# Mixture of experts with two towers on one core: order of the transfers and of the gates around the first expert's second layer

## What is computed

```python
h = relu(einsum('bi,eio->beo', x, eW1) + eb1)      # x: 512 x 1024, eW1: 8 x 1024 x 1024
h = relu(einsum('beh,eho->beo', h, eW2) + eb2)     # eW2: 8 x 1024 x 512
expert_out = einsum('beh,eho->beo', h, eW3) + eb3  # eW3: 8 x 512 x 256
gates = softmax(einsum('bi,tie->bte', x, gW) + gb, axis=-1)   # 2 tasks, 8 experts
tin = einsum('bte,bed->btd', gates, expert_out)
th = relu(einsum('btd,tdh->bth', tin, tW1) + tb1)
th = relu(einsum('bth,tho->bto', th, tW2) + tb2)
out = sigmoid(einsum('bth,tho->bto', th, tW3) + tb3)[..., 0]  # 512 x 2
```

## Time and profile before

| | |
|---|---|
| median of 3 runs | 576.89 us (575.41 to 577.55) |
| profiled execution | 576.8 us, span 575.0 us |
| mean granted clock of TensorE | 0.997 |
| TensorE busy | 567.6 us, 99% |
| VectorE busy | 454.9 us, 79% |
| ScalarE busy | 310.7 us, 54% |
| GpSimd busy | 99.8 us, 17% |
| moved by DMA | 86.87 MB, 151 GB/s on average |

### The profile page before, as it was taken

The page is one execution under the profiler, slowest core; times in us unless marked ns, Lnnn a source line. Parts: engine busy times, 40 slices in busy tenths (PEclk is TensorE's granted clock), DMA queues, the critical chain, the costliest instruction groups (busy, mean ns, idle before and its releaser), DMA issues.

```text
span 575.0 us, 8534 instructions
## 1 busy us (share of the span) xinstructions
PE 567.6 (99%) x2883; PEld 478.4 (83%) x2883; DVE 454.9 (79%) x576; ACT 310.7 (54%) x422; POOL 99.8 (17%) x106
## 2 busy tenths in 40 slices
PE   9999989999999999999999999999999999999998
PEld 6788878888888888888888888888888888888776
DVE  7998559976898758976799759977699767998493
ACT  3484546724764365633665346733757346654553
POOL 0200411033201511033100431024110332004000
PEclk9999989999999999999999999999999999999999
DMA  9824784368635765466744577266744676416100
GB/s 322 225 85 149 186 210 101 136 161 232 152 106 170 190 155 142 146 165 164 201 97 154 149 201 178 77 183 184 165 125 146 164 186 185 122 73 204 52 1 0
DMA packets 39774, 86.87 MB, mean 151 GB/s; under 512 B 3521, under 2 KB 8769, under 8 KB 39762
## 3 DMA queue, kind: packets, MB, share of 16 engines
q1 hardware_dynamic: 29762, 66.50, 34.4%
q0 software_dynamic: 9856, 19.96, 20.3%
q10 hardware_dynamic: 144, 0.26, 0.2%
HBM read 86.68 MB, written 0.04 MB: 151 GB/s over the span
## 4 chain that ended last, share of the span: by engine, by line
PE 84%; DVE 3%; DMA 2%; issue 2%; ACT 1%; POOL 1%; ACTq 0%; POOLq 0%; DVEq 0%
PE psum L487 31%; PE psum L490 16%; PE psum L347 12%; PE psum L348 12%; PE psum L349 12%; DMA w_raw<-eW_pairs 2%; DVE w_lo L998 1%; DVE h_lo L1014 1%; POOL scratch L1414 0%; DVE scratch L1091 0%; ACT w_hi L953 0%; ACT h_hi L819 0%; ACT scratch L988 0%; DVE scratch L1069 0%; POOL gates_dram L1417 0%
## 5 line engine op out<-in xcount | busy, mean ns | idle before, releaser
L998 DVE TENSOR_TENSOR w_lo<-w_raw,w_hi 128x1024 fp32r<-128x1024 f32 (+2 forms) x108 | 137.8, 1280 | 19.2 <-ACT w_hi L782 12.0
L347 PE MATMUL psum<-h_hi,w_hi 128*128 128x512 f32 (+1 forms) x340 | 131.8, 388 | 0.8 <-DVE h_lo L1014 0.8
L487 PE MATMUL psum<-t_both,w_hi 128*128 128x512 f32 x480 | 131.6, 396 | 0.0
L348 PE MATMUL psum<-h_lo,w_hi 128*128 128x512 f32 (+1 forms) x340 | 131.6, 387 | 0.0
L349 PE MATMUL psum<-h_hi,w_lo 128*128 128x512 f32 (+1 forms) x340 | 131.4, 387 | 0.0
L487 PE MATMUL psum<-x_both,w_hi 128*128 128x512 f32 x360 | 98.7, 396 | 2.2 <-ACT scratch L803 2.2
L487 PEld LDWEIGHTS psum<-t_both,w_hi 128*128 128x128 f32 x480 | 83.1, 190 | 11.6
L1401 POOL DMA_DIRECT2D w_raw<-eW_pairs x30 | 25.9, 865 | 343.8 <-DMA w_raw<-eW_pairs 343.1
L1014 DVE SCALAR_TENSOR_TENSOR h_lo<-scratch,h_hi 128x512 fp32r<-128x512 f32 (+1 forms) x66 | 66.8, 1013 | 23.4 <-ACT scratch L845 19.0
L490 PEld LDWEIGHTS psum<-t_both,w_lo 128*128 128x128 f32 x480 | 73.8, 189 | 10.3
L490 PE MATMUL psum<-t_both,w_lo 128*128 128x256 f32 x480 | 76.4, 281 | 0.0
(11 more groups left out here) (100 smaller groups left out, 582.2 us busy)
## 6 DMA issues: line engine op xcount, KB each, us to landing
w_raw<-eW_pairs SPq DMA_DIRECT2D x30, 768.0 KB, 4.2
w_raw<-eW SPq DMA_DIRECT2D x40, 512.0 KB, 4.0
scratch<-eW_pairs SPq DMA_DIRECT2D x30, 256.0 KB, 4.8
w_raw<-eW_pairs SPq DMA_DIRECT2D x30, 256.0 KB, 5.1
w_raw<-eW_pairs POOLq DMA_DIRECT2D x30, 256.0 KB, 4.9
scratch<-eW_pairs POOLq DMA_DIRECT2D x30, 256.0 KB, 6.5
scratch<-gates_dram POOLq DMA_DIRECT2D x8, 512.0 KB, 5.6
w_raw<-tW SPq DMA_DIRECT2D x4, 512.0 KB, 4.2
```

Source lines behind the costliest of these rows:

```text
L347: pe.matmul(bank, weights_hi, moving_hi, start=first, stop=False)
L348: pe.matmul(bank, weights_hi, moving_lo, start=False, stop=False)
L487: pe.matmul(whole, weights(w_hi, kk), moving(kk), start=(starts and kk == 0), stop=False, skip_group_check=True)
L998: dve.tensor_tensor(wide(w_lo, slots), raw, wide(w_hi, slots).bitcast(F32), ALU.subtract).then_inc(slot_ready, 1)
```

## The change

Four things are done together.

1. GpSimd issues the accumulating DMAs of (1,1) right behind those of (1,0), ahead of the memsets and the gates' trip.
2. SyncE orders the blocks of (1,0) behind the low part of piece 0 instead of piece 1. For that, piece 1 moves from raw unit 0 to unit 3, piece 2 to unit 2, and piece 3 to unit 3 behind piece 1, so it is ordered once the low part of piece 1 is done.
3. `turn_gates` moves on TensorE from ahead of layer 2 of expert 0 to behind P4 of pair 3, inside it.
4. VectorE's order around it is another one.

```diff
-FIRST_W2_UNIT = [1, 0, 3, 2]
+FIRST_W2_UNIT = [1, 3, 2, 3]
+FIRST_PER_UNIT = [1 + FIRST_W2_UNIT.count(u) for u in range(UNITS)]
...
@@ sync @@
-            for n, what in enumerate([("G3", 2), ("G4", 2), ("G3", 3), ("G4", 3)]):
-                sp.wait_ge(slot_ready, split(0, *what))
-                load_w2(0, n)
-
-            sp.wait_ge(slot_ready, split(0, "W2", 1))
+            sp.wait_ge(slot_ready, split(0, "G3", 2))
+            load_w2(0, 0)
+            sp.wait_ge(slot_ready, split(0, "G3", 3))
+            load_w2(0, 1)
+
+            sp.wait_ge(slot_ready, split(0, "W2", 0))
             load_blocks(1, 0)
             load_a22(1, 0)
+            sp.wait_ge(slot_ready, split(0, "G4", 3))
+            load_w2(0, 2)
+            sp.wait_ge(slot_ready, split(0, "W2", 1))
+            load_w2(0, 3)
@@ tensor @@
                     if first and (n, m) == (2, 0):
                         last_product(e, PAIRS - 1)
+                        turn_gates()
...
             pair(0, 3)
-            turn_gates()
             layer2(0)
@@ scalar @@
                     u = FIRST_W2_UNIT[i]
-                    act.wait_ge(landed[u], 2 * DMA)
+                    act.wait_ge(landed[u], (1 + FIRST_W2_UNIT[:i + 1].count(u)) * DMA)
...
@@ vector @@
             upper_fold(0, 2)
             lower_fold(0, 2)
+            w2_lo(0, 0)
             c11_sum(0, 3)
...
-            w2_lo(0, 0)
+
             g4_lo(0, 3)
+            c12_sum(0, 3)
+            c21_fold(0, 2)
+            c22_sum(0, 3)
+            pair_h1_lo(0, 2)
+            w2_lo(0, 1)
+
             dve.wait_ge(exp_done, 1)
...
-            c12_sum(0, 3)
-            c22_sum(0, 3)
-            c21_fold(0, 2)
-            pair_h1_lo(0, 2)
-            w2_lo(0, 1)
+            upper_fold(0, 3)
+            lower_fold(0, 3)
             w2_lo(0, 2)
             dve.wait_ge(gates_turned, 1)
             dve.tensor_copy(turned[0:T * E, :], banks[BANK_GATES][0:T * E, :]).then_inc(gated_ready, 1)
-            upper_fold(0, 3)
-            lower_fold(0, 3)
             c21_fold(0, 3)
@@ gpsimd @@
             sum_blocks(1, 0)
+            sum_blocks(1, 1)
 
             pool.wait_ge(t_ready, NX)
...
-                for i in range(1, PAIRS):
+                for i in range(2 if e == 1 else 1, PAIRS):
```

More of the change, by code:

```diff
@@ L821, in w3_split @@
             def w3_split(e):
-                act.wait_ge(landed[W3_UNIT], (2 + PER_UNIT[W3_UNIT] * (e - 1) + 1) * DMA)
+                act.wait_ge(landed[W3_UNIT], (FIRST_PER_UNIT[W3_UNIT] + PER_UNIT[W3_UNIT] * (e - 1) + 1) * DMA)
                 wait_slots(e, W3_AT, 2)
@@ L828, in w2_hi @@
                     u = FIRST_W2_UNIT[i]
-                    act.wait_ge(landed[u], 2 * DMA)
+                    act.wait_ge(landed[u], (1 + FIRST_W2_UNIT[:i + 1].count(u)) * DMA)
                 else:
                     u = W2_UNIT[i]
-                    act.wait_ge(landed[u], (2 + PER_UNIT[u] * (e - 1) + W2_UNIT[:i + 1].count(u)) * DMA)
+                    act.wait_ge(landed[u], (FIRST_PER_UNIT[u] + PER_UNIT[u] * (e - 1) + W2_UNIT[:i + 1].count(u)) * DMA)
                 wait_slots(e, W2_AT + 2 * i, 2)
@@ L940, in _ @@
                 w2_hi(e, 3)
-            act.wait_ge(landed[LAST_W3_UNIT], (2 + PER_UNIT[LAST_W3_UNIT] * (E - 1) + 1) * DMA)
+            act.wait_ge(landed[LAST_W3_UNIT], (FIRST_PER_UNIT[LAST_W3_UNIT] + PER_UNIT[LAST_W3_UNIT] * (E - 1) + 1) * DMA)
             act.wait_ge(out3_done, OUT3 * (E - 1))
@@ L947, in tower_hi @@
                 u = TOWER_UNIT[i]
-                act.wait_ge(landed[u], (2 + PER_UNIT[u] * (E - 1) + (2 if u == LAST_W3_UNIT else 1)) * DMA)
+                act.wait_ge(landed[u], (FIRST_PER_UNIT[u] + PER_UNIT[u] * (E - 1) + (2 if u == LAST_W3_UNIT else 1)) * DMA)
                 if i < 3:
```

## The result

The changed kernel took 572.88 us (median of 10 runs, 572.65 to 573.45); the kernel before, in the same session, 576.27 us (median of 10 runs, 573.92 to 577.55). The ratio is 0.9945 with a 95% interval of 0.993 to 0.996: faster by 0.55%, by the medians 3.4 us. The profiled execution has a span of 570.9 us against 575.0.

The account below looks back on a forecast made before the run. TensorE, busy 99% of the 575.0 us span, was taken as the bound, so only idle or low-clock time could be won: 2.37 + 1.66 = 4.03 us off 576.8 to 576.9 gives 572.9 us, range 571.4 to 575.6.

Parts of the forecast that it names:

- The wait of 2.37 us: TensorE at P3 of (1,0), held by the late p5_take on ScalarE: 2.37 us lost, expected to go entirely.
- The 1.66 us of lower clock: P3 and P7 behind TensorE's wait in expert 1: 4.45 us instead of 2.79 at clock 0.60; 1.66 us to win.
- The sum of 4.03 us: Expert 1 on TensorE: 2.37 us of wait plus 1.66 us of lower clock come off, nothing is added.
- longest here: Landings of accumulating DMAs: 9.33 us claimed as the longest; being slower would need 13 to 16 us for (1,2).
- The single cause: GpSimd's queue: the gates' trip ahead of the accumulating DMAs of (1,1) makes p5_take late; moving them ahead wins 4.03 us.
- This alone wins nothing on TensorE: SyncE's queue: ordering (1,0) at about 44.9 instead of 53.04 gains nothing by itself, since (1,0) was not late.
- The trip as a fixed 9.25 us: GpSimd, second accumulating DMA to broadcast: 9.25 us kept unchanged, so broadcast at 75.6 and DMA of (1,2) at 76.1.
- The slower one: GpSimd's gates' trip holds back (1,2), delaying P7 of (1,1): 578 to 580 us, chance 0.06.
- The short wait: DMA of (1,2) or (1,1) lands half a microsecond to two late: 574 to 576 us, chance 0.12.
- the wait that stays: Piece 3 lands so late that (1,1) is no earlier than 77.7: 576.9 us, chance 0.06.
- Zero for the transposes: The gates' four transposes on TensorE, moved to about 55.1 inside layer 2: at most 0.60 us in either place, nothing net.

Follow-up runs that it names:

- the first four experiments: Kernel before with GpSimd's order alone, 573.28 us; changed kernel without it, 573.21; kernel before with SyncE's order and raw units alone, 574.03; with VectorE's and TensorE's orders alone, 573.26.
- The run with seven copies: Changed kernel with seven 128x256 copies on ScalarE ahead of p5_take of pair 0 in each of the loop's seven experts; one run, 591.07 us.
- the loads held back: Kernel before, SyncE's plain loads of (1,2) waiting until the first accumulating DMA of (1,1) has landed; 574.33 us, ratio 0.9983.
- the delayed trip: Changed kernel with eight more memsets on GpSimd between the accumulating DMAs of (1,1) and the gates' trip; 575.1 us, ratio 0.9988.

## Why the prediction was right, and where it was not

**The wait of 2.37 us.** It was there and it went: no wait at P3, and P3 1.40 us behind P6. The times of the schedule came as worked out: (1,0) ordered at 44.77 (44.9 foreseen), piece 1 ready at 51.5 (51.8), piece 3 landed after 6.9 us (6.8) and ready at 60.76 (60.8), the DMA of (1,1) at 65.23 (65.3), the broadcast at 75.04 (75.6), the DMA of (1,2) at 75.59 (76.1), landed at 82.3 (81 to 85.4). Only the landing of (1,1) was quicker than the 5 to 6 us: 4.1. The sum of 4.03 us against the profiled execution came out as 4.1 (575.0 to 570.9). The 6.9 us of piece 3 beside the accumulating DMAs agree with the sentence of the Trainium skill (DMA: Bandwidth & Descriptors, section "SWDGE vs HWDGE vs iDMA") on queues that are served in turn. The "longest here" of 9.33 us was the longest of the first DMAs of a pair only; the second of (1,1) took 10.8 in the same trace. Nothing hung on that.

**The 1.66 us of lower clock: the mis-sized term.** The prediction took them as part of every run, because the profiled execution had them. They are not. Of the 31 runs of the kernel before that the first four experiments share, 14 had a mean granted clock of 0.997, as the profiled one, with a median of 576.97 us, and 17 had 1.000, with a median of 575.02. The difference is 1.95 us, the 1.66 and 0.3 more. The changed kernel had 1.000 in all its 10 runs. On the chip on which the changed kernel ran again (573.05 us), 7 runs of before with 0.997 had a median of 577.16 and 11 with 1.000 one of 575.36. So the gain is about 4.1 us against a run like the profiled one, 2.3 us against the others, and 3.4 between the medians of the main comparison, not 4.0: 0.55% instead of 0.70%. The 2.3 us are near the 2.37 of the wait alone; no profile shows such a run of before, so that its wait is as long is argued, not shown. The run with seven copies shows the same thing within one execution. The median of 572.9 was met all the same: both terms were taken off a profiled execution that had both, and after the change little is left to be uncertain (its runs spread over 0.8 us, where the 31 of before spread over 4.3). With a profile of one of the other runs as the base, 1.66 us would have been taken off a time that did not hold them; that the profile fell on such a run is luck.

**The single cause: a step that failed.** "This alone wins nothing on TensorE", of the earlier order of (1,0), was wrong, and so was the weight given to GpSimd's order as the one remedy. GpSimd's order alone wins the time, VectorE's and TensorE's alone win it too, and SyncE's alone 2.0 of the 2.8 us by the medians. The old wait needed a coincidence: the DMA of (1,1) had to leave just behind the broadcast and just ahead of the 1 MB of (1,2). With the loads held back it landed after 6.5 us, with the broadcast 7.4 us ahead after 6.0. A queue's order was only one way into that collision, and each part of the change takes the DMA out of it.

**The trip as a fixed 9.25 us.** "That stretch is work and landings of the trip alone" was wrong too: some 4 us of it depend on what else is in flight. The stores took 6.0 us to land before and 5.2 in the changed kernel, with two accumulating DMAs ahead of them and 1 MB of plain loads issued near them, and 1.8 in two runs and 2.3 with SyncE's order alone, without that 1 MB. Which of the two holds them is not separated: in the changed kernel the first of them landed at 73.6, when both accumulating DMAs had been down since 71.2, so it is not those alone. It did no harm here, because in the changed kernel the stores have the same kinds of neighbours as before (8.7 us from 66.38 to 75.04), but with it the expectation for the delayed trip put the DMA of (1,2) 4.5 us too late.

**The rivals.** The slower one, the trip that holds back (1,2), has its place right: delaying the trip by 8.4 us, and holding the plain loads back, both brought the wait out at P7 of (1,1). Its price was too high for two reasons: the trip shrinks when it starts late, and the clock did not fall behind the waits of 1.03 and 1.49 us in these profiles. The short wait and the wait that stays did not come.

**Zero for the transposes.** The four stand at 54.97 (55.1 foreseen), and nothing waits for them.

What stays open: how much of the spread of the kernel before at full clock (573.3 to 576.2 us) is the length of the wait and how much the start of the kernel, since no profile fell on a run near its lower end; and which of VectorE's and TensorE's moves in the third part did it. That was not tried.

## What to carry to other kernels

A DMA that lands late may be late because of what is issued a microsecond after it, together with what stands ahead of it in its queue; before reordering a queue, look at what shares the DMA engines with it, since a lead of 2 us can be worth 6. Judge the price of a wait by several runs: the part that comes from the granted clock was there in about half of them only, and a profile shows one. And a stretch that ends with a landing is no constant: ask what else is in flight.

## What the runs showed of the hardware

- Two stores of 16 KB from GpSimd's queue took 1.8 us to land in two traces and 2.3 in a third, with no 1 MB of plain loads issued near them. In five traces they took 5.2 to 6.0 us, with the second of two accumulating DMAs of 256 KB issued 2.3 us ahead and 1 MB of plain loads between 2.5 us ahead and 0.2 behind. The two neighbours are not separated.
- An accumulating DMA of 256 KB took 4.1 to 5.2 us in the rows of the table with neither neighbour within 2 us, 5.9 to 6.8 us with a 512 KB broadcast 0.55 us ahead, 4.9 us with 1 MB of plain loads 0.9 us behind alone, 9.3 us with the broadcast and the 1 MB 1.1 us behind, and 8.1 to 9.0 us where the 1 MB was issued within 0.6 us of it.
- The granted clock behind a wait of TensorE, in the profiled executions: 1.00 behind each of seven delays of about 0.4 us (idle gaps of 0.14) and behind waits of 1.03 and 1.49 us; 0.59 and 0.68 over 4.2 us behind two of seven waits of 1.94 us, 1.00 behind the other five; 0.50 to 0.65 behind each of seven waits of 3.73 us.
- The first eight matmuls on the experts' weights take 2.14 us in some executions and 2.95 in others, which moves all that follows. TensorE's timeline, first of the changed kernel and then of the one without GpSimd's order:

```profile
4.95 2.14 PE L477 MATMUL psum<-x_both,w_hi 128*128 128x512 f32 x8 [0.28 <-ACT w_hi L856]
```

```profile
4.83 2.95 PE L477 MATMUL psum<-x_both,w_hi 128*128 128x512 f32 x8
```
